# The value products of a head group in one burst instead of four

## Chip, cores and metric

The kernel runs on one core of a Trainium2 chip. The metric is the device time of one execution in microseconds (us).

## The reference, cut to what matters

Input x is (4, 512, 128): four sequences of T = 512 positions and C = 128 channels. Two blocks follow one another, both with 16 heads and causal softmax attention:

```python
x = x + layernorm(attn1(layernorm(x), Wq, Wk, Wv, Wo))      # rope, head size 8
x = x + layernorm(ffn(layernorm(x), ...))
# ffn: latent attention (head size 64: 32 plain, 32 rope; keys and values from a
#      16-wide latent), then a mixture of 8 experts (top 2) and a shared expert
scores = q @ k.T * scale; scores = where(causal, scores, -inf)
out = softmax(scores) @ v
```

Everything is float32; the change touches only `softmax(scores) @ v`, the value products, of both attentions.

## The kernel before

**Groups.** The attention work is cut into 32 head groups n = 0..31, each of four heads of one sequence and one layer. In order of n they are: layer 1 for n = 0..11 and 16..19, layer 2 for 12..15 and 20..31. A group passes three stages, and the stages of three groups are interleaved:

- *for the maximum*: TensorE computes the lower triangle of scores with the query on the partitions (`scores_for_max`, `products`: L490 in layer 1, L493 in layer 2, and a mask product L495 for the diagonal block). A group takes 11 fills of a 2 KB bank; they alternate between only two banks, 0 and 1. VectorE reduces each fill to negated row maxima (L1124). A fill f waits until fill f-2 has been reduced (`fill_read`). VectorE then splits the maxima into low-precision parts (`split_max`, L1147 to L1157), TensorE turns them (`turnmax`, L608, L611), ScalarE copies, and a DMA puts them into the query stack.
- *for the exponential*: two groups later, `scores_for_exp` computes the scores with the key on the partitions (L516 in layer 1, L522 in layer 2), 10 units of a bank, over three banks; ScalarE takes the exponential of each (L785) into PG. A unit waits for the exponential of the unit three before it.
- *values*: one group later still, `values(n - 1, j)` for key block j = 0..3 multiplies the exponentials with V (L565). One j is 4 products, one for each head, each into its own 32 of the 128 partitions of one bank; each stands as two instructions in the trace (so x8). They cover 512, 384, 256 and 128 query columns for j = 0, 1, 2, 3. They wait for GpSimd's zeroing of the upper triangles (`causal`, L1070 in layer 1, L1077 in layer 2), and j = 0 also for all exponentials and for VectorE's division of the group before (`on_ready`). The last product signals `pv`; ScalarE copies the bank to OT (L791), TensorE turns OT back (`turn_out`, L572), VectorE divides (L1165, L1174).

**The order on TensorE** is written out in `main(n, hh)`, called for heads hh = 0..3 of each step n. Within a head the slots i = 0..3 run in turn: a unit for the exponential of group n, a fill for the maximum of group n + 2, then, at four slots, one j of `values(n - 1, j)`. Heads 0, 1, 2, 3 hold 2, 3, 2, 4 fills and 2, 3, 2, 3 units. So a step runs, with E a unit, M a fill and Vj the value products of block j:

```
hh 0: E M, E M            hh 1: E M V0, E M V1, E M V2
hh 2: E M V3, E M         hh 3: E M, E M, E M, M, turn_out
```

After each head, `stream` adds the stages of the rest of the model that the list `BESIDE` puts there (projections, norms, rotation, experts); `turnmax` of the next group always stands behind head 1.

**VectorE's order** at head 0 of a step is: split part 0, reciprocal, reduce; split part 1, division, reduce; split parts 2 and 3 (layer 1 only), and then the reductions of head 1. Step 32 has no units or fills left: V0, V1 and V2 follow one another, and V3 comes behind the expert work that `BESIDE` lists at (32, 1).

Of the kernel before, what the change touches and what calls it, by code (L numbers as in the profile page):

```python
# [25 lines left out]
NT = T // P  # L26
# [9 lines left out]
TWO_ONES = 1.0 + 0x3F80 / 2.0 ** 23  # L36
NEG = -1e30
FILLS = 11
VALUES_AT = ((1, 0), (1, 1), (1, 2), (2, 0))
UNITS = 10  # L40

CAUSAL_ORDER = (0, 1, 2, 3)
# [14 lines left out]
NG = G * len(PHASES)  # L57
# [155 lines left out]
def block_program(nc, x, wqkv, wo1, wkva, wq_nope, wq_rope, wkvb, wo2, ln1w, ln2w, wgate, gbias, wgu, wgu_s, wd,  # L213
                  wd_s, ident, masks, rope1, ropek, ropeq, rank, expert_rows, out):
    with ExitStack() as ctx:
# [270 lines left out]
        def _(pe):  # L486
# [10 lines left out]
            def fills_of(hh):  # L497

                return 2 * hh + hh // 2, 2 + hh % 2 + hh // 3

            def scores_for_max(n, hh, i):
                h = HG * (n % G) + hh
                f = n * FILLS + fills_of(hh)[0] + i
                if f >= 2:
                    pe.wait_ge(fill_read, f - 1)
                bank = ps[:, f % 2, :]
                heads = (1, 1, 2, 4)[i]
                for j in range(heads):
                    w = P * (4 - i)
                    mm = products(bank[:, w * j:w * j + w], n, h - heads + 1 + j, 3 - i, 4 - i)  # L510
                mm.then_inc(score_fill, 1)
# [14 lines left out]
            def scores_for_exp(n, hh, i):  # L526

                h = HG * (n % G) + hh
                u = n * UNITS + 5 * (hh // 2) + 2 * (hh % 2) + i
                if hh == 0 and i == 0:  # L530
                    pe.wait_ge(m_stacked[n % G], 16 * (n // G + 1))
                if u >= 3:
                    pe.wait_ge(exp_done, u - 2)
                bank = ps[:, ST0 + u % 3, :]
                if LAYER[n] == 2:
                    mm = scores_t2(bank, n, *BLOCKS2[u % UNITS])
                else:
                    tiles = (((0, T, h, 0),), ((0, 3 * P, h, 1), (3 * P, T, h, 3)),
                             ((0, 256, h - 1, 2), (256, T, h, 2)))[i]
                    for lo, hi, head, j in tiles:  # L540
                        mm = scores_t1(bank[:, lo:hi], head, j)
                mm.then_inc(st_ready, 1)

            def values(n, j):

                pe.wait_ge(causal, NT * (n + 1) if LAYER[n] == 2 else NT * n + CAUSAL_ORDER.index(j) + 1)
                if j == 0:
                    pe.wait_ge(exp_done, UNITS * (n + 1))
                    if n:
                        pe.wait_ge(on_ready, n)  # L550
                    if n % G == 0:
                        pe.wait_ge(v1_ready if LAYER[n] == 1 else v2_ready, SEQ[n] + 1)
                for hh in range(HG):
                    h = HG * (n % G) + hh
                    out = ps[32 * hh:32 * hh + 32, BK_O, P * j:T]
                    if LAYER[n] == 1:
                        v = V1[:, j, h, :]
                        p = (PG[:, n % 2, 2 * hh, :], PG[:, n % 2, 2 * hh + 1, 0:3 * P],
                             PG[:, n % 2, 8 + hh // 2, 256 * (hh % 2):256 * (hh % 2) + 256],
                             PG[:, n % 2, 2 * hh + 1, 3 * P:T])[j]  # L560
                    else:
                        v = V2[:, SEQ[n] % 2, j, :]
                        out = out.rearrange("d (i q) -> d i q", q=P)
                        p = PG[:, n % 2, PLACE2[j]:PLACE2[j] + NT - j, P * hh:P * hh + P]
                    mm = pe.matmul(out, v, p, start=(j == 0), stop=(j == NT - 1), skip_group_check=True)  # L565
                if j == NT - 1:
                    mm.then_inc(pv, 1)

            def turn_out(n):
                pe.wait_ge(ot_ready, n + 1)  # L570
                for t in range(NT):
                    mm = pe.transpose(ps[:, BK_O, P * t:P * t + P], OT[:, P * t:P * t + P], ident_sb[:])  # L572
                mm.then_inc(o_turned, 1)

            def main(n, hh):

                if hh == 0 and n + 2 < NG:
                    m = n + 2
                    if m == 0:
                        pe.wait_ge(consts_ready, CONSTS)  # L580

                    if LAYER[m] == 1:
                        pe.wait_ge(stack1_in[m % G], 32 * (SEQ[m] + 1))
                    else:
                        pe.wait_ge(stack2_in[m % G], 128 * (SEQ[m] + 1))
                        pe.wait_ge(k_low, SEQ[m] + 1)
                for i in range(4):
                    if 0 <= n < NG and i < 2 + hh % 2:
                        scores_for_exp(n, hh, i)
                    if n + 2 < NG and i < fills_of(hh)[1]:  # L590
                        scores_for_max(n + 2, hh, i)
                    if 1 <= n <= NG and (hh, i) in VALUES_AT:
                        values(n - 1, VALUES_AT.index((hh, i)))
                if hh == 3 and 1 <= n <= NG:
                    turn_out(n - 1)

# [155 lines left out]
            def y3part(b, part):  # L752
# [9 lines left out]
                if part == 4:  # L762
                    mm.then_inc(bank_full, 1)

            stream(main, dict(
                y3part=y3part, turnmax=turnmax, x1T=turn_tile("x1T"), q1=q1, v1=v1, wprod=wprod, wturn=wturn, o1T=o1T,
                o1y=outputs("o1y", lambda b: ONT_AFTER["o1T", b], [wo1_sb[:]]), x2T=turn_tile("x2T"), kst=kst, latv=latv,
# [692 lines left out]
```

## Time and profile before

| | |
|---|---|
| median of 3 runs | 652.36 us (646.97 to 653.94) |
| the profiled execution | 647.78 us, its span 646.1 us |
| TensorE busy | 549.5 us, 85% of the span |
| VectorE, ScalarE, GpSimd busy | 396.2, 309.1, 212.8 us |
| mean granted TensorE clock | 0.943 |

The span is the time from the first to the last instruction in the profile; 1.7 us of the profiled execution lie around it. Busy time of an engine is the union of its instructions. A line such as L565 is the line of the kernel's source that issued an instruction.

### The profile page before, as it was taken

The page shows a single profiled execution, that of the slowest core. Times are in us where ns is not written, and L with a number is a line of the kernel's source. Part 1 is how long each engine was busy: PE and PEld are TensorE (multiplying, and loading weights), DVE is VectorE, ACT ScalarE, POOL GpSimd, SP SyncE. Part 2 cuts the span into 40 slices and gives each one's busy share as a digit, 9 for nine tenths or more (in the row PEclk, how much of TensorE's full clock was granted, in tenths as well). Part 3 has the DMA queues.
Part 4 walks back from the last instruction along what each step waited for, and adds up shares of the span by engine and source line. Part 5 has one row for each costly group of instructions (what it writes and reads, how often), then busy time and mean ns, then how long its engine had stood idle before and what let it go on. Part 6 is the DMA issues. An engine that isn't in the chain of part 4 may idle for free.

```text
span 646.1 us, 10027 instructions
## 1 busy us (share of the span) xinstructions
PE 549.5 (85%) x3586; PEld 308.5 (48%) x3586; DVE 396.2 (61%) x932; ACT 309.1 (48%) x589; POOL 212.8 (33%) x276
## 2 busy tenths in 40 slices
PE   2877989787879897799878998999999999899873
PEld 1833435434435454444435555545575446643632
DVE  6368887576767555565765576756656765434463
ACT  2223756575455752466435555554435432564221
POOL 4544543242633731650352311414331110220101
PEclk9576999999899898899989999999999999999998
DMA  8461214211343462201561122125404120000000
GB/s 225 107 171 42 77 38 97 68 53 58 136 113 62 98 156 90 100 35 59 107 166 65 57 51 47 41 80 128 89 14 91 27 51 1 19 2 0 1 17 16
DMA packets 28545, 46.15 MB, mean 71 GB/s; under 512 B 5104, under 2 KB 14352, under 8 KB 27920
## 3 DMA queue, kind: packets, MB, share of 16 engines
q1 hardware_dynamic: 28496, 45.52, 27.4%
q8 instruction: 28, 0.46, 0.3%
q14 instruction: 21, 0.17, 0.1%
HBM read 27.22 MB, written 17.83 MB: 70 GB/s over the span
## 4 chain that ended last, share of the span: by engine, by line
PE 57%; DVE 20%; ACT 6%; issue 5%; SPq 5%; DMA 3%; POOL 3%; POOLq 0%; DVEq 0%; ACTq 0%
PE ps L565 11%; PE ps L522 9%; PE ps L628 8%; DVE NM L1124 6%; PE ps L493 5%; PE ps L490 4%; PE ps L495 4%; PE ps L516 2%; DVE terms L1224 2%; PE ps L650 2%; PE ps L748 2%; DVE stats L1108 2%; PE ps L674 2%; PE ps L572 1%; PE ps L611 1%
## 5 line engine op out<-in xcount | busy, mean ns | idle before, releaser
L1124 DVE TENSOR_REDUCE NM<-ps 128x1 f32<-128x512 f32 (+3 forms) x352 | 219.5, 639 | 120.0 <-PE ps L495 113.0
L785 ACT ACTIVATE PG<-ps 128x512 f32<-128x512 f32 x320 | 181.4, 596 | 160.9 <-PE ps L522 93.6
L522 PE MATMUL ps<-QS,K 128*128 128x512 f32 x320 | 118.6, 455 | 0.6 <-DMA QS<-MP 0.6
L495 PE MATMUL ps<-maskb,identb 128*128 128x128 bf16 x512 | 111.1, 235 | 0.0
L565 PE MATMUL ps<-PG,V 128*32 128x512 f32 (+3 forms) x1024 | 98.4, 458 | 6.7 <-POOL PG L1070 5.2
L493 PE MATMUL ps<-K,QS 96*128 96x256 f32 (+3 forms) x256 | 84.8, 375 | 15.4 <-DVE NM L1124 15.1
L490 PE MATMUL ps<-KS,QS 96*128 96x256 bf16 (+3 forms) x256 | 74.7, 327 | 20.5 <-DVE NM L1124 19.3
L495 PEld LDWEIGHTS ps<-maskb,identb 128*128 128x128 bf16 x512 | 52.4, 102 | 38.7 <-issue 31.4
L522 PEld LDWEIGHTS ps<-QS,K 128*128 128x128 f32 x320 | 51.6, 195 | 39.6 <-issue 21.1
L516 PE MATMUL ps<-QS,KS 128*128 128x128 bf16 (+3 forms) x256 | 63.8, 311 | 6.3 <-DMA QS<-scr 4.2
L1029 POOL TENSOR_TENSOR whole<-terms 128x512 f32<-128x512 f32 x28 | 35.4, 1273 | 101.4 <-DVE terms L1224 65.1
L974 POOL TENSOR_TENSOR rstd<-ve,half 128x4 f32<-128x4 f32 x20 | 20.4, 1021 | 141.5 <-DVE ve L1116 105.4
L493 PEld LDWEIGHTS ps<-K,QS 96*128 96x128 f32 x256 | 50.5, 200 | 30.5 <-DVE NM L1124 24.2
L1077 POOL TENSOR_SCALAR_AFFINE_SELECT PG<-PG 128x512 f32<-128x512 f32 x64 | 40.1, 644 | 73.3 <-ACT PG L785 72.4
L1070 POOL TENSOR_SCALAR_AFFINE_SELECT PG<-PG 128x512 f32<-128x512 f32 x64 | 38.7, 638 | 36.7 <-ACT PG L785 36.2
L490 PEld LDWEIGHTS ps<-KS,QS 96*128 96x128 bf16 x256 | 26.1, 103 | 51.8 <-DVE NM L1124 40.3
L628 PE MATMUL ps<-QS,KS 128*128 128x512 f32 (+1 forms) x80 | 40.3, 622 | 0.4 <-DVE QS L1355 0.2
L516 PEld LDWEIGHTS ps<-QS,KS 128*128 128x128 bf16 x256 | 19.9, 100 | 43.1 <-issue 16.6
L565 PEld LDWEIGHTS ps<-PG,V 128*32 128x32 f32 x1024 | 20.8, 109 | 28.6 <-issue 14.9
L1058 POOL TENSOR_TENSOR QC<-whole,QC 128x512 fp32r<-128x512 f32 x16 | 20.4, 1276 | 37.0 <-ACT QC L885 37.0
L1351 DVE SCALAR_TENSOR_TENSOR KS<-QS,ps 128x512 f32<-128x512 f32 (+1 forms) x20 | 13.7, 685 | 19.3 <-ACT QS L952 19.0
L1224 DVE TENSOR_TENSOR terms<-ps,ropeq_sb 128x512 f32<-128x512 f32 x32 | 20.5, 684 | 6.5 <-POOLq L1061 4.5
(153 smaller groups left out, 658.6 us busy)
## 6 DMA issues: line engine op xcount, KB each, us to landing
scr<-QC SPq DMA_DIRECT2D x24, 512.0 KB, 3.1
QS<-scr SPq DMA_DIRECT2D x64, 128.0 KB
QS<-scr_q SPq DMA_DIRECT2D x16, 288.0 KB
KS<-scr_k SPq DMA_DIRECT2D x16, 288.0 KB
QS<-scr SPq DMA_DIRECT2D x64, 64.0 KB
scr_k<-room SPq DMA_DIRECT2D x40, 64.0 KB, 2.1
scr_q<-room SPq DMA_DIRECT2D x24, 64.0 KB, 2.1
x<-in_x SPq DMA_DIRECT2D x4, 256.0 KB, 5.8
```

What stands on the lines that cost most here:

```text
L490: pe.matmul(dst, QS1[0:MROW, h, P * i:P * i + P], KS1[0:MROW, h, 0:P * k], start=True, stop=False)
L493: pe.matmul(dst, QS2[0:MROW, h, P * i:P * i + P], K1[0:MROW, SEQ[n] % 2, 0:P * k], start=True, stop=False)
L495: return pe.matmul(dst[:, P * (k - 1):P * k], identb[:], maskb[:, 0, :], start=False, stop=True)
L516: return pe.matmul(dst, KS1[:, h, q0:q0 + P], QS1[:, h, q0:T], start=True, stop=True)
L522: mm = pe.matmul(bank.rearrange("p (h q) -> p h q", h=HG), keys[:, SEQ[n] % 2, P * j:P * j + P], QS2[:, heads, P * i:P * i + P], start=(ke ...
L565: mm = pe.matmul(out, v, p, start=(j == 0), stop=(j == NT - 1), skip_group_check=True)
L628: pe.matmul(bank(u)[0:rows, :], w, xT, start=True, stop=True).then_inc(bank_full, 1)
L785: act.activation(PG[:, n % 2, unit_place(LAYER[n], (u + k) % UNITS), :], ps[:, ST0 + (u + k) % 3, :], ACT.Exp, scale=scale).then_inc(exp_d ...
L1029: pool.tensor_tensor(whole[:, j % 2, :], terms[:, j % 2, 0, :], terms[:, j % 2, 1, :], ops[part % 2])\
L1070: pool.affine_select(blocks, blocks, pattern=[*heads, [1, P]], compare_op=ALU.is_ge, fill=0.0, base=0, channel_multiplier=-1).then_inc(cau ...
L1077: pool.affine_select(blocks, blocks, pattern=[[0, HG], [1, P]], compare_op=ALU.is_ge, fill=0.0, base=0, channel_multiplier=-1).then_inc(ca ...
L1124: dve.tensor_reduce(dst, src, AX.X, ALU.max, negate=True).then_inc(fill_read, 1)
```

## The change

`VALUES_AT` held the four slots of V0 to V3; it is now the one slot (head 1, i = 2), at which all four blocks are issued in a row, 16 products. Nothing else differs: the same products with the same operands and waits.

```diff
-VALUES_AT = ((1, 0), (1, 1), (1, 2), (2, 0))
+VALUES_AT = (1, 2)
...
-                    if 1 <= n <= NG and (hh, i) in VALUES_AT:
-                        values(n - 1, VALUES_AT.index((hh, i)))
+                    if 1 <= n <= NG and (hh, i) == VALUES_AT:
+                        for j in range(NT):
+                            values(n - 1, j)
```

The step becomes:

```
hh 0: E M, E M            hh 1: E M, E M, E M V0 V1 V2 V3
hh 2: E M, E M            hh 3: E M, E M, E M, M, turn_out
```

## Rows read from the trace of the kernel before

**Rows 1.** The page's first part: busy time, share of the span, instructions.

```profile
PE 549.5 (85%) x3586; PEld 308.5 (48%) x3586; DVE 396.2 (61%) x932; ACT 309.1 (48%) x589; POOL 212.8 (33%) x276
```

**Rows 2.** The chain that ended last, shares by engine.

```profile
PE 57%; DVE 20%; ACT 6%; issue 5%; SPq 5%; DMA 3%; POOL 3%; POOLq 0%; DVEq 0%; ACTq 0%
```

**Rows 3.** Windows of mostly layer 1, then layer 2: length, busy (instructions), clock, DMA.

```profile
60.00:227.00 167.00, 140.97 (x1114) 72.47 (x1111) 117.96 (x283) 103.09 (x201) 72.75 (x102) 0.96 0.30 78
...
366.00:560.00 194.00, 181.75 (x1138) 107.06 (x1137) 118.57 (x276) 92.28 (x171) 47.85 (x67) 1.00 0.24 54
```

**Rows 4.** TensorE's waits, two in 60 to 227, one in 366 to 560.

```profile
PE ps L490 <- DVE NM L1124: 9.1, 10, 2.7
...
PE ps L565 <- POOL PG L1070: 3.3, 3, 2.2
...
PE ps L493 <- DVE NM L1124: 6.7, 9, 1.3
```

**Rows 5.** Timeline of TensorE, step 3, a layer-1 step: start, duration, operation.

```profile
93.34 1.06 PE L565 MATMUL ps<-PG,V 128*32 128x512 f32 x8 [0.52 <-POOL PG L1070]
94.33 0.39 PE L516 MATMUL ps<-QS,KS 128*128 128x384 bf16 x2
...
94.88 0.85 PE L565 MATMUL ps<-PG,V 128*32 128x384 f32 x8
95.66 0.39 PE L516 MATMUL ps<-QS,KS 128*128 128x256 bf16 x2
...
96.33 0.64 PE L565 MATMUL ps<-PG,V 128*32 128x256 f32 x8
...
97.70 0.42 PE L565 MATMUL ps<-PG,V 128*32 128x128 f32 x8
98.06 0.39 PE L516 MATMUL ps<-QS,KS 128*128 128x384 bf16 x2
...
98.51 0.38 PE L516 MATMUL ps<-QS,KS 128*128 128x512 bf16 x1
```

**Rows 6.** Timeline of TensorE, step 32, three blocks in a row.

```profile
595.03 2.14 PE L565 MATMUL ps<-PG,V 128*32 128x512 f32 x24
597.10 0.50 PE L628 MATMUL ps<-CT,erow 128*128 128x512 f32 x1
597.53 0.42 PE L565 MATMUL ps<-PG,V 128*32 128x128 f32 x8
```

**Rows 7.** Timeline of TensorE, steps 14 and 15, layer-2 steps.

```profile
283.38 0.71 PE L522 MATMUL ps<-QS,K 128*128 128x512 f32 x2
...
284.14 0.71 PE L522 MATMUL ps<-QS,K 128*128 128x512 f32 x2
...
289.28 1.06 PE L565 MATMUL ps<-PG,V 128*32 128x512 f32 x8
290.28 0.73 PE L522 MATMUL ps<-QS,K 128*128 128x512 f32 x2
...
291.18 0.85 PE L565 MATMUL ps<-PG,V 128*32 128x384 f32 x8
```

**Rows 8.** Timeline of VectorE, reductions of head 1's first fill, steps 1, 3, 15, 27, 29.

```profile
68.89 0.68 DVE L1124 TENSOR_REDUCE NM<-ps 128x1 f32<-128x512 f32 x1
...
94.43 0.68 DVE L1124 TENSOR_REDUCE NM<-ps 128x1 f32<-128x512 f32 x1
...
290.00 0.68 DVE L1124 TENSOR_REDUCE NM<-ps 128x1 f32<-128x512 f32 x1
...
508.12 1.15 DVE L1124 TENSOR_REDUCE NM<-ps 128x1 f32<-128x512 f32 x2
...
548.13 1.14 DVE L1124 TENSOR_REDUCE NM<-ps 128x1 f32<-128x384 f32 x2
```

**Rows 9.** Step 11: a long wait of V0, and the window behind it.

```profile
213.75 1.92 PE L565 MATMUL ps<-PG,V 128*32 128x512 f32 x8 [2.24 <-POOL PG L1070]
...
213.70:217.20 3.50, 3.45 (x16) 1.01 (x20) 0.48 (x2) 1.15 (x3) 3.32 (x5) 0.52 0.44 97
```

## The prediction

> **What bounds the kernel now.** I read the busy times first: TensorE is busy 85% of the span, no other engine over 61% [rows 1]. The chain that ended last agrees: 57% of it is TensorE, 20% VectorE [rows 2]. So TensorE's order matters, with VectorE as the second hand. The windows by stage separate two regimes [rows 3]: in 60 to 227 us, nearly all layer 1, TensorE is busy 141.0 of 167 us (84%); in 366 to 560 us, layer 2, 181.8 of 194 us (94%). What fills the rest is in the table of waits [rows 4]: in the first stretch TensorE waits 9.1 us for the reductions before a fill and 3.3 us for GpSimd's zeroing before V0; in the second 6.7 us for the reductions. (These are idle times beyond the modelled ends of matmuls; the true wait is longer.) In the timeline the reader should see where a step waits: around V0 to V3 TensorE runs without a break, and the waits for VectorE lie in heads 3 and 0, where fills are dense. The value products give VectorE time to catch up.
>
> **What a visit to the value products costs.** In step 3 the starts tell the occupation [rows 5]: V0 holds TensorE 94.33 - 93.34 = 0.99 us, V1 95.66 - 94.88 = 0.78, V3 98.06 - 97.70 = 0.36. That is 0.21 us for each 128 columns (0.99 - 0.36 over three) and about 0.14 fixed. Step 32 shows that the fixed part belongs to leaving [rows 6]: V0, V1, V2 in a row hold it 597.10 - 595.03 = 2.07 us, nine times 0.215 plus 0.14 once. Going in costs too: a unit and a fill of the same sizes take 98.51 - 98.06 = 0.45 us ahead of more scores, 94.88 - 94.33 = 0.55 ahead of V1 [rows 5]; in layer 2 0.76 (284.14 - 283.38) against 0.90 (291.18 - 290.28) [rows 7]. A visit thus costs 0.14 + 0.10 to 0.14, say 0.27 us, on top of its columns. The change removes three of four visits: 0.8 us a step, 25 us over steps 1 to 31 (3.8%) if all of it reached the end.
>
> The rule behind this is in the Trainium skill, "TensorEngine Tiling (Array Packing)", Key Properties: changing the tiling mode, not just the tile, drains TensorE. The trace agrees, as the value products use 32 columns of the array and the scores 128, with the 0.27 us above. By this rule alone the sum would be the whole 25 us, about 623 us for the profiled execution.
>
> **What the burst delays.** V0, V1 and V2 no longer stand between the fills of head 1, and these fills wait for VectorE. The critical one is the third fill of head 1. It uses the bank of the first, so it needs that one's reduction done. With V0 and V1 gone ahead of it, TensorE could issue it at (relative to the old start of V0) -0.10 + 0.45 + half a slot of 0.45 = 0.57 us in layer 1, and -0.10 + 0.80 + 0.57 = 1.27 us in layer 2, whose unit takes longer. The end of the reduction is known from the trace of before, as nothing ahead of it moves [rows 8]: in step 3 it is 94.43 + 0.68 = 95.11, which is 1.77 after V0; in step 15 290.68, 1.40 after. VectorE is late there because head 0 gives it two reductions, the splits and the division. I read this for all 29 steps with fills, the first and last of them in rows 8: in the 15 of layer 1 the mean is 1.54 us after V0 (ends -0.03 and 3.84), in the 14 of layer 2 1.40 us (eight of them at 0.93 or less, the longest 4.06).
>
> Layer 1: clipping at zero and with 0.06 us for the signal, the new wait sums to 17 us over 15 steps, of which 1.7 us is there already. Saved are 15 x 0.81 = 12 us. Net +3. Moreover V3 (0.36 us and its visit) used to stand between the two fills of head 2. From there to head 0 VectorE works almost without a gap in layer 1, so taking V3 away buys only the gaps it closes, about 0.2 of 0.46 us a step: +3 more. Against that, at steps 11 and 18 V0 waits for GpSimd, 2.24 us in the first and about as long in the other, and right after the first wait the granted clock is 0.52 (the 1.2 GHz level) for 3.5 us, in which V0 takes 1.92 us instead of 1.06 [rows 9, 5]. Two slots (about 1 us) of that wait now hold fills, and the clock may stay up: -3 together. Layer 1 comes to +3.
>
> Layer 2: 14 steps with fills and two without. Saved are 16 x 0.81 = 13 us. The new waits are 0.2, 0.8, 0.6, 0.9, 0.5 and 2.9 us (step 27, where VectorE does expert work up to 508.1 [rows 8]), less 1.0 us already waited there: +5. In three steps VectorE runs gapless through head 2, where 0.5 us each is lost again: +1.5. Layer 2 comes to -6.5.
>
> **The rest.** In step 32 V3 no longer stands behind an expert product of 0.43 us [rows 6], and the last copy waits for it: -0.5 us. The burst itself holds TensorE 10 x 0.215 + 0.14 = 2.3 us; VectorE has at most two fills (1.25 us) and ScalarE three units to work off in it, so both idle about a microsecond, which costs nothing by itself as they're idle between slots today. `turnmax` and the work of head 1 in BESIDE stood behind V2 and now stand behind V3 too: 0.2 us of columns later, less the visits saved, so a little earlier where nothing waits. The wait for the zeroing of all four blocks moves to one place; the last block is zeroed at most 1.7 us after the old V0, and V3 comes at least 1.9 us into the burst, so it binds nowhere. `pv` comes earlier. No DMA and no SP or GpSimd step moves. New waits of up to 2.9 us in steps 8, 17 and 27 may let the clock fall as in step 11; bounded by 0 and 1.7 us each (3.5 us at half the clock), I take +1.5 in all.
>
> **Sum.** +3 - 6.5 - 0.5 + 1.5 = -2.5 us: 645.3 us for the profiled execution of 647.78. The median of the runs shown is 652.36, 0.7% above the profiled one, so I forecast 650 on that basis. About 1% (6.5 us) is what a measurement of this kernel can tell from no change.
>
> **The rivals.**
> (A) *TensorE decides throughout*: the drains saved reach the end. For it: 94% busy in layer 2 and no idle time around V0 to V3. Against: the fills of head 1 must wait for reductions that end 1.4 to 1.5 us after V0 on average. With layer 2 and the GpSimd waits in full but layer 1 at break-even: -13 - 3 = -16, to 636; with everything, 627. Chance 0.25.
> (B) *Two fill banks decide*: the step becomes a ring of VectorE's reductions from head 2 through the first fill of head 1, then third fill, burst, `turnmax`, first fill of head 2 on TensorE, in which VectorE idles. In layer 1 the part up to head 2 gets longer by (reduction end + 0.06 + 2.9) - 3.76 us, that is 0.7 us a step or 11 us, and if delays in ScalarE's queue or VectorE's side work widen it to the 14 layer-2 steps at half that, +5, with 3 us of slow clock: about +15 beyond layer-2 savings that vanish, 667. It is decided by whether VectorE has spare time between head 2 and head 0: it turns slower as soon as the new wait at the third fill exceeds 0.8 us in most steps (in before 10 of 29 by my reading). For it: 9.1 us of waits for reductions in layer 1 already. Against: VectorE is busy only 61%. Chance 0.2.
> (C) *My forecast*: the two nearly cancel, between 643 and 658. Chance 0.55.
> A second rule of the Trainium skill speaks for B: the same page, PSUM Bottleneck, says that tiling speeds up TensorE but not the evacuation of PSUM, so that the copy may become the bottleneck. The trace agrees only in heads 3 and 0 of layer 1.
>
> **How the numbers follow.** Forecast 650, the likeliest case. The range leaves out the outer third of A and the outer half of B, under 2 in 10: 634 to 664. Faster by over 1% (below 645.8) is A and the lower edge of C, 0.33; slower by over 1% (above 658.9) is B and the upper edge of C, 0.23; within 1% 0.44.
>
> **What the changed profile would show.** x32 runs of L565 of about 2.3 us, one a step, and the busy time of L565 down by some 13 us if the fixed part of leaving is real. Waits of L490 for L1124 just ahead of the burst, about 1 us in layer-1 steps and near none in most layer-2 steps. No slow clock at steps 11 and 18. The stretch 366 to 560 shortened by some 5 us, the stretch 60 to 227 about equal. I would be wrong if VectorE's reduction of head 1's first fill ended much earlier or later against TensorE than today, as its backlog is carried from step to step, or if clock falls came at other steps.

## The result and the profile after

The changed kernel takes 662.97 us (median of 4 runs, 662.45 to 670.58), the kernel before 653.15 us in the same comparison (646.97 to 655.77). The ratio is 1.0196, with a 95% interval of 1.0144 to 1.0247: the burst makes the kernel 2% slower. I had forecast 650 us and no change that can be told; the range ended at 664. Here and below the medians take in every run, but the ratios leave out one that counts as slow, the profiled run of the burst at (1, 0), which lies 1.6% above the fastest of its kernel.

The profiled execution of the changed kernel is the slowest of its four runs, 670.58 us with a span of 668.5 us; 662 to 663 us is its usual time. Differences between the two profiled spans (22.5 us) are therefore larger than the change's own 10 us, and the text below says which part is which.

The first part of its page and the shares of the chain that ended last, beside rows 1 and 2:

```profile
PE 551.6 (83%) x3586; PEld 325.8 (49%) x3586; DVE 393.3 (59%) x932; ACT 305.7 (46%) x589; POOL 212.1 (32%) x276
...
PE 53%; DVE 24%; ACT 7%; issue 5%; POOL 4%; SPq 3%; DMA 3%; DVEq 0%; POOLq 0%; ACTq 0%
```

TensorE's share of the chain is down from 57 to 53% and VectorE's up from 20 to 24% [rows 2]. The value products did get cheaper and no longer wait; first the line of the kernel before, then that of the changed one (busy us, mean ns, then idle time ahead of it):

```profile
L565 PE MATMUL ps<-PG,V 128*32 128x512 f32 (+3 forms) x1024 | 98.4, 458 | 6.7 <-POOL PG L1070 5.2 <-DVE room L1174 1.0 <-DVE ON L1174 0.3
```

```profile
L565 PE MATMUL ps<-PG,V 128*32 128x512 f32 (+3 forms) x1024 | 84.7, 476 | 0.0
```

The busy time fell by 13.7 us, as worked out (13 us), and the 5.2 us of waits for GpSimd are gone. What took their place stands in the table of waits, TensorE's rows for VectorE's reductions over the whole span (total, times, longest), before and then after:

```profile
PE ps L490 <- DVE NM L1124: 19.3, 23, 2.7
PE ps L493 <- DVE NM L1124: 15.1, 14, 3.7
```

```profile
PE ps L490 <- DVE NM L1125: 29.3, 34, 3.2
PE ps L493 <- DVE NM L1125: 23.6, 20, 4.2
```

34.4 us have become 52.9. Where they lie is seen in the timeline of step 3, TensorE and then VectorE (start, duration; in brackets the idle time ahead), against rows 5 and 8:

```profile
94.12 0.39 PE L490 MATMUL ps<-KS,QS 96*128 96x512 bf16 x1 [0.40 <-DVE NM L1125]
...
95.20 0.34 PE L490 MATMUL ps<-KS,QS 96*128 96x384 bf16 x1 [0.41 <-DVE NM L1125]
...
96.90 0.28 PE L490 MATMUL ps<-KS,QS 96*128 96x256 bf16 x1 [1.10 <-DVE NM L1125]
...
97.45 3.89 PE L565 MATMUL ps<-PG,V 128*32 128x512 f32 x32
101.16 0.39 PE L609 MATMUL ps<-identb,MB 128*12 128x128 bf16 x4
```

```profile
95.06 0.59 DVE L1152 CAST MB<-MRest 128x16 bf16<-128x16 f32 x1
95.69 0.56 DVE L1154 TENSOR_TENSOR MB<-MRest,MB 128x16 bf16<-128x16 f32 x1
96.17 1.14 DVE L1125 TENSOR_REDUCE NM<-ps 128x1 f32<-128x512 f32 x2
97.56 0.69 DVE L1125 TENSOR_REDUCE NM<-ps 128x2 f32<-128x512 f32 x1 [0.25 <-PE ps L495]
```

The third fill of head 1 starts at 96.90, right when VectorE's reduction of the first one, begun at 96.17, ends (a single one of 512 takes 0.68 us [rows 8]). All three fills of head 1 now wait, of which the first did so before the change too; then TensorE spends its burst while VectorE, after one last reduction at 97.56, has nothing. The burst here takes 3.71 us (101.16 - 97.45), not 2.3: it fell into a stretch at the lower clock, as the window shows (clock in the third column from the end):

```profile
97.20:100.60 3.40, 3.40 (x23) 0.96 (x24) 0.80 (x2) 0.00 (x0) 0.00 (x0) 0.50 0.00 0
```

Step 15 is one with units of layer 2. The burst has about the length worked out (308.64 - 306.46 = 2.18 us to `turnmax`), and the fill ahead of it waits some 0.25 us. In 8 of the 14 such steps that wait is 0.2 us or less:

```profile
305.21 0.71 PE L522 MATMUL ps<-QS,K 128*128 128x512 f32 x2
306.02 0.28 PE L490 MATMUL ps<-KS,QS 96*128 96x256 bf16 x1
...
306.46 2.36 PE L565 MATMUL ps<-PG,V 128*32 128x512 f32 x32
308.64 0.39 PE L609 MATMUL ps<-identb,MB 128*12 128x128 bf16 x4
```

The windows from the start of one turning back to that of another (steps 1, 11, 15, 19 and 32), and from the last to the end, give the loss by stage (length, busy TensorE, weight load, VectorE, ScalarE, GpSimd, then clock). Before:

```profile
76.64:223.78 147.14, 122.97 (x968) 63.33 (x965) 101.72 (x240) 88.11 (x171) 63.49 (x87) 0.95 0.31 82
223.78:299.19 75.41, 67.01 (x415) 36.49 (x414) 41.86 (x96) 39.97 (x78) 29.79 (x41) 0.93 0.28 85
299.19:363.41 64.22, 54.35 (x403) 29.20 (x401) 42.13 (x91) 32.97 (x64) 19.89 (x23) 0.95 0.39 101
363.41:598.67 235.26, 220.74 (x1362) 126.59 (x1361) 140.31 (x339) 113.33 (x211) 56.43 (x80) 1.00 0.21 48
598.67:646.05 47.38, 29.14 (x148) 19.56 (x148) 21.53 (x70) 10.02 (x22) 5.96 (x7) 0.91 0.04 12
```

After:

```profile
77.10:238.57 161.47, 129.58 (x967) 70.24 (x965) 100.24 (x240) 86.26 (x169) 63.31 (x87) 0.88 0.28 74
238.57:314.17 75.60, 65.59 (x415) 38.70 (x414) 41.74 (x96) 40.04 (x80) 29.65 (x41) 0.91 0.28 86
314.17:381.98 67.81, 52.49 (x404) 30.18 (x401) 40.87 (x91) 32.62 (x65) 19.69 (x23) 0.95 0.38 96
381.98:616.68 234.70, 214.86 (x1362) 129.14 (x1361) 139.46 (x338) 112.14 (x211) 56.26 (x80) 0.99 0.20 48
616.68:668.54 51.86, 33.08 (x148) 22.58 (x148) 22.16 (x71) 10.02 (x22) 5.95 (x7) 0.79 0.04 11
```

The layer-1 stretches (first and third) are 14.3 and 3.6 us longer; the layer-2 stretches are 0.2 longer and 0.6 us shorter; and the end is 4.5 us longer at a clock of 0.79 instead of 0.91. The end does the same work in the same order, but it isn't out of the change's reach: in step 32 V3 now comes ahead of an expert product. The last result is turned back earlier after V0 than before, yet VectorE is then at two multiplications for the experts (L1368) and takes its reciprocal (L1166) only behind both:

```profile
617.42 0.69 DVE L1368 TENSOR_TENSOR QS<-QS,ps 128x512 f32<-128x512 f32 x1 [0.22 <-DVE QS L1368]
618.26 0.26 DVE L1166 RECIPROCAL rec<-ps 128x16 f32<-128x16 f32 x1
```

From V0 of step 32 to the product that reads the division it takes 5.4 us, and took 5.2. Of the eight profiles of this study in which V3 follows V2 directly in step 32, five have an end of 51.9 to 52.1 us at a clock of 0.79 and three one of 46.7 to 48.2; the ten others lie between 45.8 and 48.7 us. So the long end goes with the changed order, but doesn't always come with it.

### The profile page after: what moved, and what is told of

Same layout as the page of the kernel before. It is cut to its first block, busy times and chain, and to the rows that moved or that the text cites. A ratio compares the mean times of both kernels' runs of the same rounds, so it can differ in the third digit from the quotient of the medians.

```text
span 668.5 us, 10027 instructions
## 1 busy us (share of the span) xinstructions
PE 551.6 (83%) x3586; PEld 325.8 (49%) x3586; DVE 393.3 (59%) x932; ACT 305.7 (46%) x589; POOL 212.1 (32%) x276
## 4 chain that ended last, share of the span: by engine, by line
PE 53%; DVE 24%; ACT 7%; issue 5%; POOL 4%; SPq 3%; DMA 3%; DVEq 0%; POOLq 0%; ACTq 0%
PE ps L565 11%; DVE NM L1125 8%; PE ps L629 8%; PE ps L522 7%; PE ps L493 5%; PE ps L490 4%; PE ps L495 3%; DVE terms L1225 3%; PE ps L651 2%; PE ps L749 2%; PE ps L675 2%; DVE stats L1109 2%; PE ps L572 2%; PE ps L516 2%; PE ps L612 1%
## 5 line engine op out<-in xcount | busy, mean ns | idle before, releaser
L1125 DVE TENSOR_REDUCE NM<-ps 128x1 f32<-128x512 f32 (+3 forms) x352 | 217.2, 637 | 123.2 <-PE ps L495 113.5
L786 ACT ACTIVATE PG<-ps 128x512 f32<-128x512 f32 x320 | 178.3, 596 | 110.0 <-PE ps L522 61.3
L493 PE MATMUL ps<-K,QS 96*128 96x256 f32 (+3 forms) x256 | 88.2, 388 | 24.1 <-DVE NM L1125 23.6
L490 PE MATMUL ps<-KS,QS 96*128 96x256 bf16 (+3 forms) x256 | 76.7, 335 | 31.4 <-DVE NM L1125 29.3
L565 PE MATMUL ps<-PG,V 128*32 128x512 f32 (+3 forms) x1024 | 84.7, 476 | 0.0
L516 PE MATMUL ps<-QS,KS 128*128 128x128 bf16 (+3 forms) x256 | 67.2, 326 | 8.2 <-DMA QS<-scr 3.9
L493 PEld LDWEIGHTS ps<-K,QS 96*128 96x128 f32 x256 | 52.1, 206 | 43.0 <-DVE NM L1125 36.5
L490 PEld LDWEIGHTS ps<-KS,QS 96*128 96x128 bf16 x256 | 26.5, 105 | 68.0 <-DVE NM L1125 55.4
L565 PEld LDWEIGHTS ps<-PG,V 128*32 128x32 f32 x1024 | 31.9, 117 | 48.9 <-issue 39.7
L1071 POOL TENSOR_SCALAR_AFFINE_SELECT PG<-PG 128x512 f32<-128x512 f32 x64 | 38.6, 636 | 41.8 <-ACT PG L786 41.3
L516 PEld LDWEIGHTS ps<-QS,KS 128*128 128x128 bf16 x256 | 22.9, 106 | 24.0 <-issue 5.4
L803 ACT ACTIVATE MP<-ps 12x512 bf16<-12x512 bf16 x16 | 9.4, 585 | 53.2 <-PE ps L609 53.1
L806 ACT ACTIVATE MP<-ps 8x512 f32<-8x512 f32 x16 | 9.4, 586 | 51.4 <-PE ps L612 51.4
```

What stands on the lines that cost most here:

```text
L490: pe.matmul(dst, QS1[0:MROW, h, P * i:P * i + P], KS1[0:MROW, h, 0:P * k], start=True, stop=False)
L493: pe.matmul(dst, QS2[0:MROW, h, P * i:P * i + P], K1[0:MROW, SEQ[n] % 2, 0:P * k], start=True, stop=False)
L516: return pe.matmul(dst, KS1[:, h, q0:q0 + P], QS1[:, h, q0:T], start=True, stop=True)
L786: act.activation(PG[:, n % 2, unit_place(LAYER[n], (u + k) % UNITS), :], ps[:, ST0 + (u + k) % 3, :], ACT.Exp, scale=scale).then_inc(exp_d ...
L1071: pool.affine_select(blocks, blocks, pattern=[*heads, [1, P]], compare_op=ALU.is_ge, fill=0.0, base=0, channel_multiplier=-1).then_inc(cau ...
L1125: dve.tensor_reduce(dst, src, AX.X, ALU.max, negate=True).then_inc(fill_read, 1)
```

## The experiments

Each ratio is to the kernel before on the same chip, with its 95% interval; the median in brackets has that of the kernel before beside it.

**Which steps lose.** `VALUES_AT` is again the tuple of four slots, and the burst is issued by layer:

```diff
+ for j in range(NT):
+     if 1 <= n <= NG and (hh, i) == ((1, 2) if n < NG and LAYER[n] == 1 else VALUES_AT[j]):
+         values(n - 1, j)
```

> Burst only in the 15 steps whose units are of layer 1 (1 to 11, 16 to 19); spread as before elsewhere. Theory W+C (the waits before the third fill of head 1 and the falls of the clock that they bring, both of layer 1): the whole loss and more is here, +8 to +16 us against the kernel before. Theory R (the ring of two fill banks slows every step alike): half of the loss, about +5.

Measured 1.0169, 1.0106 to 1.0233 (662.81, before 652.1): +10.7 us, the whole loss.

For layer 2 the condition is `n == NG or LAYER[n] == 2`.

> Burst only in the 16 steps whose units are of layer 2, and in step 32; spread as before in layer 1. Theory W+C: near the kernel before or faster, -6 to +1 us. Theory R: about +5 us.

Measured 0.9978, 0.9945 to 1.0012 (652.68): no change that can be told. The loss belongs to the 15 layer-1 steps; R falls. The first and the third stretch in the profile of the layer-1 burst matter for the question of the clock:

```profile
76.47:229.62 153.15, 119.76 (x954) 66.53 (x965) 98.85 (x240) 85.58 (x169) 63.44 (x87) 0.94 0.30 78
...
303.54:375.65 72.11, 56.53 (x396) 34.61 (x401) 42.19 (x91) 32.54 (x64) 19.70 (x23) 0.88 0.35 90
```

With the same order of work in these steps as the changed kernel the first takes 153.15 us at a clock of 0.94, not 161.47 at 0.88. It is still 6.0 us above the kernel before at nearly the same clock (0.95). The third is 7.9 us above it, at 0.88 against 0.95.

Steps 2 to 7 run at the full clock in this profile as in that of before, so the clock has no part in their difference (before, then the layer-1 burst):

```profile
76.64:154.53 77.89, 66.56 (x576) 33.95 (x574) 55.73 (x129) 50.48 (x98) 29.29 (x44) 1.00 0.23 61
```

```profile
76.47:156.94 80.47, 63.49 (x568) 35.36 (x573) 54.68 (x129) 49.59 (x98) 29.30 (x44) 1.00 0.22 59
```

They lose 2.6 us, 0.43 us a step.

**Is it the clock?**

```diff
+ if 1 <= n < NG and (hh, i) == (1, 2) and LAYER[n] == 1:   # ahead of the fill
+     pe.wait_ge(on_ready, n - 1)                            # for n >= 2
+     for _ in range(6):
+         pe.matmul(ps[:, BK_O, 0:2 * P], identb[:], maskb[:], start=True, stop=True)
```

> The burst, with 6 products of 256 columns (0.64 us, their result overwritten) put ahead of the third fill of head 1 in the 15 layer-1 steps, where TensorE waits about 1 us. Theory C (most of the loss is the granted clock, which falls after these waits): the clock falls of layer 1 vanish and the time comes down by 8 to 15 us from the changed kernel, to about 650. Theory W (the waits alone): 0 to +4 us against the changed kernel, as the products fit into the wait or lengthen it.

Measured 1.014, 1.0095 to 1.0184 (660.4): 2.6 us under the changed kernel's median, with intervals that overlap. Work put into the wait costs nothing that can be told, which fits the wait being there, but it brings back little. Its profile says why. First and third stretch:

```profile
77.43:228.86 151.43, 123.12 (x1014) 71.91 (x1025) 99.67 (x240) 84.57 (x166) 62.98 (x85) 0.97 0.30 78
...
305.98:373.77 67.79, 54.68 (x420) 33.74 (x425) 41.38 (x91) 32.55 (x65) 19.71 (x23) 0.95 0.36 96
```

The time at half clock in the two is about 16 us ((1 - 0.97) x 2 x 151 + (1 - 0.95) x 2 x 68), less than the 21 us of before and far less than the 36 us of the layer-1 burst. Still they are 7.9 us longer than before. In the layer-1 burst they are 13.9 us longer, and 8.5 of that lies in steps 10, 18 and 19 alone, where the time at half clock is 22 us instead of 8. So in the profiles some 6 us of the loss go with the lower clock, and 8 us stay without it (the products put in may themselves add a little: in steps 2 to 7 they cost 0.5 us). The four runs of the changed kernel point the same way: their mean clocks are 0.907, 0.919, 0.955 and 0.922, their times 670.6, 662.9, 662.5 and 663.0 us. At 0.955, above the 0.943 of the profiled execution of before, it is as slow as at 0.92. Only the profiled run carries a large extra loss at a low clock. C falls as the main cause; its share in the median isn't settled.

**Saving a visit without touching head 1's cover.** `VALUES_AT = ((1, 0), (1, 1), (1, 2), (1, 2))`.

> Only V3 moves, ahead to V2: three visits instead of four. The cover ahead of head 1's fills stays. If drains reach the end where nothing new waits: -0.27 x 31 = -8 us at most; if the waits at the third fill of head 3 (28 us in the kernel before) take up what V3 frees in head 2: about -2 us.

Measured 1.0, 0.9972 to 1.0028 (651.89, before 652.1). One visit less is worth nothing that can be told here. Its profile has the long end of the changed kernel, 51.9 us instead of 47.4, while its stretch from step 19 to step 32 is 2.3 us shorter.

**Is it VectorE's lateness?** All reductions of a fill read 128 columns, so the maxima leave out most of the keys:

```diff
- src, dst = ((bank, ...), (bank[:, 0:3 * P], ...), (... a=2), ...), (... a=4), ...))[i]
+ src, dst = ((bank[:, 3 * P:4 * P], ...), (bank[:, 2 * P:3 * P], ...),
+             (... a=2)[:, :, P:P + 64], ...), (... a=4)[:, :, 0:32], ...))[i]
```

> The kernel before, with each reduction of a fill reading 128 columns instead of 384 or 512 (the maxima are then taken over a part of the keys; everything else is computed as before). Its time is only the base for the next run. VectorE gets some 130 us less work; what TensorE waited for the reductions (about 50 us) should mostly go: 610 to 630 us.

> The changed kernel with the same short reductions. Theory W (the burst loses by the waits of fills for reductions, and by nothing else): with VectorE fast, only the saved visits are left, so it is 15 to 25 us faster than the run of short reductions with the blocks spread. Rival S (the burst starves ScalarE, or holds back the other stages that stand behind it): it stays slower or equal.

Spread: 0.9708, 0.9651 to 0.9765 (632.56, before 650.74). Burst: 0.9568, 0.95 to 0.9637 (624.27). With a fast VectorE the same burst is 8.3 us faster than the spread order, where it was 10 us slower: the sign turns, S falls. The gain is half of the least that W expected. The waits of L490 and L493 were still 19.4 us spread and 30.7 us in the burst (sums of two rows each); I had taken them mostly to go. The splits and the divisions of head 0 were not shortened, which may be why.

**Which reductions?** Only two are cut, in `maximum`:

```diff
+ if (hh, i) in ((0, 1), (1, 0)):
+     src = src[:, 2 * P:3 * P]
```

> The kernel before, with only the reductions of the second fill of head 0 and the first fill of head 1 cut to 128 columns (their maxima are taken over a part of the keys). Base for the next run; these two are hidden behind V0 and V1 today, so 0 to 6 us faster than before.

> The changed kernel with the same two short reductions. Each is some 0.3 to 0.4 us shorter, so the reduction on which the third fill of head 1 waits ends 0.75 us earlier. Theory W: of the 13 us of new waits there in layer 1 some 10 go, and the run comes within 3 us of its base (the changed kernel lies 10 us above its own). If the loss sat elsewhere (head 2 and 3, ScalarE, the other stages behind the burst): still some 10 us above the base.

Spread: 0.9867, 0.9823 to 0.9911 (646.88, before 652.79). Burst: 0.994, 0.9896 to 0.9985 (647.9). The gap is 1.0 us by the medians and 0.7%, some 5 us, by the ratios, whose intervals touch; uncut it is 10 (2.0%). Two reductions of eleven, those that end just before the third fill of head 1, thus carry more than half of the burst's loss; how much more, the intervals leave open. The waits of L490 and L493 are 30.8 us spread and 41.8 in the burst, so the gap between them shrank from 18.5 to 11.0 us and did not close. The base gained 6 us as well, the upper end of what I had allowed.

**Is it the burst or its place?** `VALUES_AT = (1, 0)`, one burst of 16, behind the first fill of head 1:

> The same burst of 16, behind the first fill of head 1 instead of the third. Theory W (the loss is the wait of head 1's later fills for reductions, which end about 1.5 us after the first fill): the burst of 2.3 us now covers that wait, three visits are still saved, and only V0's own waits stay: 4 to 15 us faster than the kernel before. Rival B (any burst of 2.3 us starves the other engines): as slow as the changed kernel, about +10.

Measured 0.9781, 0.9705 to 0.9857 (640.75, before 653.17): the same burst two slots earlier is 2.2% faster than the kernel before. Its timeline of step 3 (TensorE), where the second and third fill (L490 at 94.68 and 95.12) follow their units without a wait:

```profile
92.16 2.36 PE L565 MATMUL ps<-PG,V 128*32 128x512 f32 x32 [0.52 <-POOL PG L1071]
94.45 0.39 PE L516 MATMUL ps<-QS,KS 128*128 128x384 bf16 x2
94.68 0.33 PE L490 MATMUL ps<-KS,QS 96*128 96x384 bf16 x1
...
94.91 0.38 PE L516 MATMUL ps<-QS,KS 128*128 128x256 bf16 x2
95.12 0.27 PE L490 MATMUL ps<-KS,QS 96*128 96x256 bf16 x1
```

and its rows in the table of waits, whose sum, 35.4 us, is that of the kernel before (34.4):

```profile
PE ps L490 <- DVE NM L1125: 20.5, 23, 3.2
PE ps L493 <- DVE NM L1125: 14.9, 14, 4.2
```

`VALUES_AT = (1, 1)`, one slot later:

> The burst behind the second fill of head 1. That fill waits only for head 0's second reduction, which ends near V0's old start; the third fill is covered. Theory W: close to the burst behind the first fill, 8 to 13 us faster than before. If covering is gradual (each fill ahead of the burst costs the same): half-way between -13 and +10, about -1 us.

Measured 0.9828, 0.9774 to 0.9882 (644.11, before 652.79): -8.7 us. So the three places give -12.4, -8.7 and +9.8 us. The first two can't be told apart by their intervals; the step comes with the third fill, and a gradual price, which would have given about -1 us for this run, falls.

**Other places.** The burst at (3, 0), with ScalarE's copy to OT moved behind the second exponential of head 3 (and the old slots in step 32):

> The burst behind the first fill of head 3, with ScalarE's copy behind the second exponential of head 3. Theory W: it covers the wait of head 3's third fill (0.9 us a step) but leaves the fills of head 1 without cover, where about 1 us a step of layer 1 comes up: -6 to +4 us. Rival B: about +10.

Measured 0.992, 0.9891 to 0.9949 (648.08, before 653.17). The rival of these runs, that any burst of this length starves the others (it is called B there, but it is not the B of the prediction), falls with both places.

V3 alone at (3, 1), the copy moved likewise:

> Still four visits, but V3 stands behind the second fill of head 3, just ahead of the fill that waits longest for VectorE (28 us in the kernel before), and ScalarE's copy of the result follows the second exponential of head 3. Theory W: V3's 0.5 us a step goes into that wait, and head 2 gets shorter: 4 to 12 us faster than before. Rival S (the copy and turning back come too late and stall the end of head 3): equal or slower.

Measured 1.0143, 1.0074 to 1.0211 (660.86, before 650.74): slower, against W. TensorE now waits for ScalarE's copy before it can turn the result back:

```profile
PE ps L573 <- ACT OT L781: 7.7, 7, 2.7
```

V2 and V3 at (3, 1):

> V2 and V3 in one visit behind the second fill of head 3; V0 and V1 stay. Theory W: 1.1 us a step moves into a wait of 0.9 us and one visit is saved, against a third fill of head 1 that loses V2's cover only behind it, so no new wait there: 8 to 18 us faster than before. If VectorE's backlog from head 0 just moves on to head 1's fills: within 3 us of the kernel before.

Measured 0.9865, 0.9795 to 0.9935 (643.9, before 650.74): -6.8 us, below the 8 to 18 that W gave; 6.0 us of waits for the copy are in it. The same pair at (3, 0), the copy behind the first exponential:

> V2 and V3 in one visit one slot earlier than in the run that was 1.35% faster: behind the first fill of head 3, the copy behind its first exponential. TensorE's waits for the copy (6 us there) should go: 3 to 6 us faster than that run, about 1.5 to 2.3% under the kernel before. If the copy's waits only move to fills: equal to it.

Measured 0.9876, 0.982 to 0.9932 (643.14, before 653.17): no better than the run it was to beat, by the ratios, though TensorE's waits for the copy fell from 6.0 to 1.7 us. They only moved.

V0, V1 at (1, 0) and V2, V3 at (3, 0), the copy behind the second exponential of head 3:

> V0 and V1 in one visit behind head 1's first fill, V2 and V3 in one behind head 3's first: two visits saved, both congested places covered. Theory W: at least as fast as the run before it, by up to 8 us more (one more visit saved, 31 x 0.27). If V1's move from the second slot leaves the third fill of head 1 to wait: up to 5 us slower than it.

Measured 0.9804, 0.9745 to 0.9862 (639.23, before 653.17): 3.9 us under the run before it, within the 8 us expected, but the intervals overlap.

V0, V1 at (1, 0) and V2, V3 at (2, 0), ScalarE as before:

> V0 and V1 behind the first fill of head 1, V2 and V3 behind the first fill of head 2; ScalarE's copy as in the kernel before. Two visits saved, 17 us of TensorE time at most. Theory W: no fill loses its cover where VectorE is late, so 6 to 14 us faster than before. If cover in head 1 must be spread evenly: within 3 us of before.

Measured 0.972, 0.967 to 0.9771 (636.19, before 652.79): 2.8% faster than the kernel before and 4% under the changed one, the fastest of this study with every reduction in full. Its waits for reductions are below those of before, and the products' busy time is down 15 us:

```profile
PE ps L490 <- DVE NM L1125: 17.8, 22, 2.3
PE ps L493 <- DVE NM L1125: 14.4, 14, 3.3
```

```profile
L565 PE MATMUL ps<-PG,V 128*32 128x512 f32 (+3 forms) x1024 | 83.4, 443 | 6.9 <-POOL PG L1071 4.9 <-DVE room L1175 1.0 <-DVE ON L1175 0.7
```

## Why the prediction was wrong

**What a visit costs** held: 0.27 us, and L565 is busy 13.7 us less in all, with 13 us worked out for leaving. That it can reach the end is shown by the burst at (1, 0), though as 12.4 us, not 25. The Trainium skill's rule quoted there ("TensorEngine Tiling (Array Packing)", Key Properties: a change of mode drains TensorE) agrees with that. What it leaves out, who waits once the visits are merged, decided the sign.

**The place of the new wait** held: the third fill of head 1, for the reduction of the first. Counted over the timeline (start of a fill less start of the instruction ahead of it, less the usual distance of such a pair), it waits about 15 us over the 15 layer-1 steps, where I had 17, and 6.3 us in layer 2, where I had 5.9.

**The step that failed** is the sum of layer 1, "Layer 1 comes to +3". Alone it measures +10.7 us. Three of its terms were off. (1) Among the new waits of head 1 I counted only the third fill. The second one waits 2.3 us more as well, a term that I had put at nothing. The first fill of head 3 waits 2.4 us more and its third 1.2 (same count); these 3.6 us are what the "+3 more" for V3 was to cover. That term has a slip in it: a step that keeps 0.2 of 0.46 us loses 0.26, which is 3.9 us over 15 steps. (2) I took off 3 us for the waits on GpSimd at steps 11 and 18. These waits did vanish (5.2 to 0 us), but the lower clock did not: in the profile of after the bursts of both steps, at 230.0 and 354.5 us, begin at it. (3) I put the lower clock at +1.5 us for all steps. In the profile of the layer-1 burst its two layer-1 stretches hold some 15 us more at half clock than before, worth 7 us at most; with products in the wait this went, and +7.9 us stayed. In the profiled run of the changed kernel the first stretch is at 0.88 instead of 0.95, some 24 us more at half clock ((1 - 0.88) x 2 x 161 against (1 - 0.95) x 2 x 147), at most 12 us of time. So the clock explains why the profiled run is at 670 and not at 663, and a part of the median that no run here settles. With the waits as counted the sum of layer 1 would have been 15 - 1.7 - 12 + 2.3 + 3.6 = 7 us, before anything is taken off for GpSimd's waits; 7.9 us stay without the clock. What the vanished 5.2 us were worth, no run here shows by itself.

**Layer 2**, "comes to -6.5": alone -1.4 us by the ratio (interval -3.6 to +0.8). In its profile the two stretches of layer-2 steps are each 3.9 us shorter than before, the second of them at a clock of 1.00 in both, and the end is 4.6 us longer:

```profile
224.89:296.45 71.56, 62.29 (x414) 36.75 (x414) 41.65 (x96) 39.05 (x78) 29.73 (x41) 0.95 0.30 90
...
363.32:594.73 231.41, 211.56 (x1363) 128.27 (x1362) 139.34 (x338) 112.25 (x211) 56.27 (x80) 1.00 0.21 48
594.73:646.73 52.00, 33.23 (x148) 22.71 (x148) 22.14 (x71) 10.02 (x22) 5.96 (x7) 0.79 0.04 11
```

So the layer-2 steps saved about what I had worked out (7.7 us, of which the first stretch's share goes with a clock of 0.95 instead of 0.93). What took it back lies in the end, for which I had put -0.5 us, and in the layer-1 stretches, 3.8 us longer with their order unchanged. One profile shows this; whether the long end comes in most runs is open.

**The rivals.** I gave 0.55 to "the two nearly cancel" and 0.2 to B, the two fill banks. B and my forecast share the wait of the third fill; B adds that VectorE idles in the burst and is late again afterwards. The runs bear that out in part: cutting two reductions takes more than half of the loss away, and moving the burst ahead of the wait turns it into a gain. For steps 2 to 7, at full clock, my terms give +1.5 us and B's +3.4; the layer-1 burst measures +2.6. B's price for layer 1, 11 us, came out (+10.7), but some of it by the clock; its +5 for layer 2 did not (-1.4). The condition I set for it, a wait over 0.8 us at the third fill in most steps, was not met by my own count (10 of 29). It was the wrong condition: seven of the ten lie in layer 1, and that was enough for the loss there. A, all drains reaching the end, fell for this place. The rule of the Trainium skill quoted for B ("TensorEngine Tiling (Array Packing)", PSUM Bottleneck: the evacuation of PSUM may become the bottleneck) fits layer 1 only in a wide sense, as the tiling is the same in both kernels: the products got faster, and the waits for the reductions of PSUM rose from 34.4 to 52.9 us.

**Shown and not shown.** Shown: the loss is in layer 1; it needs VectorE's late reductions; it needs the burst to stand behind the third fill. Only argued: that the lower clock in the profiles of the burst follows from the new waits. Open: how much of the median is the clock; why merging V3 with V2 at (1, 2) brings nothing while two pairs at (1, 0) and (2, 0) bring 2.8%, beyond the long end that the first has in its profile; and why V3 alone at (3, 1) costs 1.4%. The waits for the copy (7.7 us) are of the size of the latter's loss, but it wasn't tried without them, and the pairs at (1, 0) and (3, 0) had 6.7 us of them and were 2% faster than before.

## What to carry to other kernels

When work is taken out from between two producers of a small ring of buffers, look up when the consumer frees the buffer that the last producer needs, and put the burst ahead of that producer, not behind it: the burst is then the cover for the wait. The same 16 products cost 2.0% behind the third fill and gained 2.2% behind the first. Add up the new waits at every fill that follows in the ring, not only at the first one that is late.

## What the runs showed of the hardware

Mean granted clock and time hardly go together here: the changed kernel took 662.5 us at 0.955 and 662.9 us at 0.919. The stretch behind step 32, with the same work in the same order, took 47.4 us at 0.91 (before), 46.8 at 0.84 (layer-1 burst) and 51.9 to 52.1 at 0.79 (changed kernel, and the burst at (1, 0) that was faster than before). So 4.5 us of a profiled span can come from where the clock's stretches fall. That isn't chance alone: 51.9 to 52.1 us stands only in profiles in which V3 follows V2 directly in step 32. But with the same order the burst at (1, 1) has a shorter one:

```profile
595.69:642.38 46.69, 29.04 (x148) 19.11 (x148) 22.12 (x71) 10.02 (x22) 5.96 (x7) 0.89 0.04 12
```

A visit of the value products, which use 32 columns of the array, between the scores, which use 128, costs TensorE about 0.27 us here. What that is worth depends on its place: 16 products in one burst cost 9.8 us in one slot and gained 12.4 us two slots earlier.
